# A fused state-space layer with a mixture of experts: both inverse roots of the row statistics in one step, those of the later chunks inside chunk 0, and a new table of places

## The reference, cut to what matters

```python
def layer(x):                        # x: (4, 1024, 256), fp32
    xn = layernorm(x)                # (x - mean) / sqrt(var + eps)
    return x + mamba(xn) + moe(xn)

def mamba(resid):                    # E = 512 channels, N = 16 states, R = 128
    rn = resid * rsqrt(mean(resid * resid) + EPS) * norm_w
    skip, x_in = rn @ skip_w.T, rn @ in_w.T
    x = silu(conv_b + causal_conv_4_taps(x_in, conv_w))
    delta = softplus(x @ wd1.T @ wd2.T + wd2_b)
    B, C = x @ wB.T, x @ wC.T
    h[l] = exp(delta[l] * A) * h[l-1] + (delta[l] * x[l]) * B[l]   # for each (e, n)
    y[l] = sum over n of h[l] * C[l]
    return resid + ((y + x * W_D) * silu(skip)) @ out_w.T

def moe(xf):                         # 8 experts, each token goes to 2 of them
    gates = softmax(xf @ Wr); scores, inds = the two smallest gates, normalised
    return sum of scores * ((silu(xf @ W1[e]) * (xf @ V1[e])) @ W2[e])
```

## Time and profile before

| | |
|---|---|
| median of 3 runs | 1356.34 us (1352.92 to 1358.64) |
| the profiled execution, its own time | 1352.63 us |
| its span | 1350.8 us |
| busy share of the span | DVE 87%, PE 83%, POOL 78%, ACT 75% |
| first scan of chunk 0, of chunk 1 | 50.86 us, 159.44 us |
| last scan ends | about 1335.9 us |

### The profile page before, as it was taken

One profiled execution on the slowest core, in us unless ns is written; L12 is line 12 of the kernel. 1 busy time (PEld: TensorE's weight loads), 2 busy tenths in 40 slices (PEclk: granted clock), 3 DMA queues, 4 the chain that ended last, 5 costly groups with the idle time before them and its releaser, 6 DMA issues.

```text
span 1350.8 us, 20706 instructions
## 1 busy us (share of the span) xinstructions
PE 1118.8 (83%) x5428; PEld 811.8 (60%) x5428; DVE 1176.3 (87%) x2147; ACT 1014.4 (75%) x2155; POOL 1054.3 (78%) x916
## 2 busy tenths in 40 slices
PE   4478476878889888889989898998989899898766
PEld 2367365655656665566666566666756666665555
DVE  5784999898989798999998899999989888989896
ACT  2898335678887887879788787978878787877863
POOL 1486278588887879789897988989888897978764
PEclk8666687789999998999999999999999999998888
DMA  7457623734444444445454354545435454434445
GB/s 215 147 194 250 249 87 87 243 127 132 135 134 145 119 141 128 133 123 149 135 141 130 120 151 127 144 135 136 139 117 144 134 140 138 134 114 129 124 139 178
DMA packets 87313, 195.37 MB, mean 145 GB/s; under 512 B 11216, under 2 KB 47312, under 8 KB 87120
## 3 DMA queue, kind: packets, MB, share of 16 engines
q1 hardware_dynamic: 69008, 171.18, 38.0%
q0 software_dynamic: 17904, 22.82, 10.3%
q10 hardware_dynamic: 288, 0.07, 0.0%
HBM read 171.36 MB, written 26.61 MB: 147 GB/s over the span
## 4 chain that ended last, share of the span: by engine, by line
PE 28%; POOL 21%; ACT 14%; issue 12%; DVE 7%; DMA 3%; DVEq 0%; POOLq 0%; ACTq 0%
POOL part L760 14%; PE yps L854 6%; ACT aexp L551 5%; PE bankX L1008 4%; PE bankH L974 4%; DVE hb L1116 4%; DVE bps L1095 3%; PE bankV L998 3%; PE bankG L879 2%; ACT tap L611 2%; POOL acc L815 2%; PE bankV L879 2%; DMA scr<-xt,idx 1%; POOL x L788 1%; POOL tap L789 1%
## 5 line engine op out<-in xcount | busy, mean ns | idle before, releaser
L760 POOL TENSOR_TENSOR part<-hb,bcr 128x512 f32<-128x512 f32 x512 | 694.2, 1406 | 188.3 <-PE yps L854 105.2
L1116 DVE TENSOR_TENSOR_SCAN hb<-aexp,carry,bps 128x256 f32<-128x256 f32 x768 | 547.3, 735 | 10.2 <-ACT aexp L551 7.8
L551 ACT ACTIVATE aexp<-delta,Am 128x256 f32<-128x256 f32 x1024 | 447.9, 505 | 35.8 <-DVE hb L1116 33.8
L854 PE MATMUL yps<-idn,part 128*128 128x128 f32 x2048 | 326.9, 292 | 141.2 <-POOL part L760 139.1
L854 PEld LDWEIGHTS yps<-idn,part 128*128 128x128 f32 x2048 | 251.6, 149 | 241.4 <-POOL part L760 180.5
L1095 DVE TENSOR_TENSOR bps<-ups,bcr 128x512 f32<-128x512 f32 x512 | 346.1, 676 | 5.1 <-DMA bcr<-brows 3.2
L1116 DVE TENSOR_TENSOR_SCAN hb<-aexp,bps 128x256 f32<-128x256 f32 x256 | 167.7, 674 | 14.8 <-ACT aexp L551 12.5
L974 PE MATMUL bankH<-w,scr 128*128 x288 | 148.1, 639 | 11.1 <-issue 8.1
L1008 PE MATMUL bankX<-w,scr 128*128 x576 | 145.0, 397 | 12.2 <-ACT scr L701 12.1
L998 PE MATMUL bankV<-v,scr 128*128 x288 | 136.8, 598 | 0.4 <-ACT tqO L656 0.4
L1008 PEld LDWEIGHTS bankX<-w,scr 128*128 128x128 f32 x576 | 108.8, 199 | 32.9 <-issue 19.4
(11 more groups left out here) (178 smaller groups left out, 1704.8 us busy)
## 6 DMA issues: line engine op xcount, KB each, us to landing
bcr<-brows SPq DMA_DIRECT2D x256, 512.0 KB
w<-in_W SPq DMA_DIRECT2D x2, 4096.0 KB, 20.9
xch<-in_x SPq DMA_DIRECT2D x16, 256.0 KB, 4.3
w<-in_x SPq DMA_DIRECT2D x4, 1024.0 KB, 10.5
xt<-scr SPq DMA_DIRECT2D x16, 256.0 KB, 2.8
acc<-scr SPq DMA_DIRECT2D x16, 256.0 KB, 2.8
v<-in_V SPq DMA_DIRECT2D x1, 4096.0 KB, 14.3
acc<-mst POOLq DMA_DIRECT2D x15, 256.0 KB
```

The lines of the kernel that those rows point to most:

```text
L551: nc.scalar.activation(aexp[:, w % EXP_SLOTS, i, :], delta[:, c % 2, e, :], ACT.Exp, scale=Am[:, e, n:n + 1]).then_inc(s_a, 1)
L760: nc.gpsimd.tensor_tensor(part[:, w % PART_SLOTS, :, :], hb[:, w % STATE_SLOTS, :, :], bcr[:, w % (2 * ROW_PAIRS), CH:2 * CH].unsqueeze(1) ...
L854: mm = pe.matmul(yps[:, s, i * P:(i + 1) * P], part[:, w % PART_SLOTS, i, s * P:(s + 1) * P], idn[:, :], start=(n == 0 and s == 0 and i == ...
L1116: v.tensor_tensor_scan(hb[:, w % STATE_SLOTS, i, :], aexp[:, w % EXP_SLOTS, i, :], bps[w % 2][:, i, :], first, ALU.mult, ALU.add).then_inc ...
```

## The change

The two inverse roots are now taken in one step. The inner norm's one is written as a function of the variance: `rs2[:, 0]` is the inverse root of var + eps, `rs2[:, 1]` that of var * (1 + eps) + eps * eps, so one Sqrt and one refinement on a tile twice as wide give both. The piece ST is split. BN, the moments of the 30 tiles, stays in the prologue, ahead of DL instead of behind it. The inverse roots of those tiles (ST) move to place 1 of chunk 0, and with them the Sqrt on ScalarE. A one-element Exp (`warm`) follows the first silu. DL of chunk 0 goes from GpSimd to VectorE. The projection of the B and C rows is a piece of its own, B5, behind B4; in the prologue as well. The router pieces have places from RA_FIRST on and reach into chunk 1, and the tables of places and of LATER change, most in chunks 0, 1 and 15.

```diff
-B_PIECES = [..., ("B3",), ("B4", 0), ("B4", 1), ("SP", 0), ("SP", 1), ("DL",)]
+B_PIECES = [..., ("B3",), ("B4", 0), ("B4", 1), ("B5",), ("SP", 0), ("SP", 1), ("DL",)]
...
-    "other": [3, 6, 7, 7, 12, 12, 12, 14, 14, 17, 17, 18, 22, 24, 24, 24, 27, 27],
+    "other": [3, 6, 7, 7, 12, 12, 12, 14, 14, 17, 17, 18, 22, 23, 23, 24, 24, 27, 27],
...
-    0: [0, 3, 4, 9, 10, 12, 13, 17, 20, 23, 25, 25, 25, 27, 27, 27, 27, 29],
+    0: [0, 3, 4, 9, 9, 12, 13, 17, 20, 24, 25, 26, 26, 26, 26, 26, 27, 27],
...
-RA_PLACES = [29, 29, 29, 30, 30, 30]
+RA_FIRST = 24
+RA_PLACES = {
+    "router": [6, 7, 7, 8, 8, 8],
+}
+ST_PLACE = 1
...
-DVE_DELTA = (2,)
+DVE_DELTA = (0, 2)
...
-    return [("B1", 0, 0)] + b2 + convs + x2 + [("B3", 0, 0), ("B4", 0, 0), ("B4", 1, 0), ("SP", 0, 0), ("SP", 1, 0), ("DL", 0, 0), ("ST",)]
+    return [("B1", 0, 0)] + b2 + convs + x2 + [("B3", 0, 0), ("B4", 0, 0), ("B4", 1, 0), ("B5", 0, 0), ("SP", 0, 0), ("SP", 1, 0), ("BN",), ("DL", 0, 0)]
...
-    "ACT": {"B4": 1, "SP": 1, "O2": 1, "B3": 2, "X2": 1, "B5": 1, "D": 1, "B2": 1},
+    "ACT": {"B4": 1, "SP": 1, "O2": 1, "X2": 1, "B5": 1, "D": 2, "B2": 1},
...
-                for step in (STAT_VAR, STAT_RMS):
-                    act.wait_ge(stat, step[g])
-                    nc.scalar.activation(sq[:, t0:t1], ta[:, t0:t1], ACT.Sqrt).then_inc(sact, 1)
-                act.wait_ge(stat, STAT_LN[g])
+                act.wait_ge(stat, STAT_VAR[g])
+                nc.scalar.activation(sq[:, :, t0:t1], ta[:, :, t0:t1], ACT.Sqrt).then_inc(sact, 1)
...
                     act.wait_ge(ld_xch[c % 2], 16 * (c // 2 + 1))
+                    if c < 2:
+                        act.wait_ge(stat, STAT_LN[c])
...
-                    nc.scalar.activation(dtT[:, :], bank["G"][:, 0:CH], ACT.Copy)
-                    act.wait_ge(conv, KE * (c + 1))
-                    nc.scalar.activation(brow, bank["G"][0:2 * N, CH:2 * CH], ACT.Copy).then_inc(free["G"], 1)
+                    nc.scalar.activation(dtT[:, :], bank["G"][:, 0:CH], ACT.Copy).then_inc(free["G"], 1)
+                elif kind == "B5":
+                    c = piece[2]
+                    wait_full(act, "G", piece)
+                    at_least(act, brow_w, 32 * c)
+                    act.wait_ge(conv, KE * (c + 1))
+                    nc.scalar.activation(brow, bank["G"][0:2 * N, 0:CH], ACT.Copy).then_inc(free["G"], 1)
...
+                if piece == ("X2", 0, 0):
+                    nc.scalar.activation(warm[:, :], db[:, 0:1], ACT.Exp)
...
+            def inverse_roots(g):
+
+                t0, t1 = GROUPS[g]
                 dve.wait_ge(bst, 2 * t1)
                 mean, var = mv[:, t0:t1, 0], mv[:, t0:t1, 1]
+                root, under, rs = (a[:, :, t0:t1] for a in (sq, ta, rs2))
+                link(v.tensor_scalar(under[:, 0, :], var, EPS, None, ALU.add))
+
+                link(v.tensor_scalar(under[:, 1, :], var, 1.0 + EPS, EPS * EPS, ALU.mult, ALU.add))
+                assert done[0] == STAT_VAR[g]
+                dve.wait_ge(sact, g + 1)
+                link(v.reciprocal(rs, root))
+                link(v.tensor_tensor(root, rs, rs, ALU.mult))
+                link(v.tensor_tensor(root, root, under, ALU.mult))
+                link(v.tensor_scalar(root, root, -0.5, 1.5, ALU.mult, ALU.add))
+                link(v.tensor_tensor(rs, rs, root, ALU.mult))
+                link(v.scalar_tensor_tensor(out=nm2[:, :, t0:t1], in0=mean.unsqueeze(1).to_broadcast([P, 2, t1 - t0]), scalar=-1.0, in1=rs,
+                                            op0=ALU.mult, op1=ALU.mult))
+                link(v.tensor_scalar(r1[:, t0:t1], rs[:, 0, :], 1.0, None, ALU.add))
```

## The result

The changed kernel took 1331.28 us (median of 4 runs, 1328.11 to 1333.41), the kernel before 1354.63 in the runs beside it (4 runs, 1352.24 to 1358.64). The ratio is 0.9824, 95% interval 0.9802 to 0.9845: 1.8% faster. The profiled execution took 1333.41 us, its span is 1331.6.

The account below looks back on a forecast made before the run. No single engine bounds the whole kernel (VectorE 87% busy, TensorE 83%); ScalarE bounds chunk 0. Terms 10.8 - 2.8 + 0.5 = 8.5 us give 1344.1 from the profiled 1352.63, 1347.8 from the median; forecast 1345, range 1332 to 1357.

Parts of the forecast that it names:

- The first statistics and the prologue: Before chunk 0's scans: statistics end 2.1 us earlier, ScalarE's exponentials start 10.8 us earlier, the first scan 9.8 earlier.
- What chunk 0 takes back: In chunk 0: a Sqrt and two table loads are new work on ScalarE, the bounding engine, costing 2.8 us.
- My upper bound of 6.3: Most that chunk 0 takes back: 2.8 + 2.2 + 1.3 us, adding VectorE's own instructions and one more load's halt.
- The end of chunk 0: Last R pieces to start of chunk 1: 4.1 us gained less 3.6 for later R pieces, net 0.5 us gained.
- RA's wait of 9.50: Before the router, VectorE waits 9.50 us for the last logits; RA one unit later was to fill it.
- the rival in which five R pieces in a row starve the scans: Chunk 0 loses the gain again through the R chain or GpSimd: 1352 us, chance 0.19.
- the 4 or more that I had made a condition: End of chunk 0: prediction is wrong if the last R piece is not earlier by 4 us or more.
- at most 4 gained, and as much lost: Chunk 1: same instructions, only about 4 us of VectorE's time idle, so counted 0, within 4 us either way.
- The rest: Chunks 1 to 15: counted at 0; chunks 2 to 14 keep the same work, bounded by 6 us either way.
- run in parallel: From chunk 2's first scan: traces keep their distance; a change above 6 us behind 254 makes the prediction wrong.
- The rival of slower steady chunks: At place 22 ScalarE waits for TensorE and VectorE runs dry, in each of 12 chunks: 1360 us, chance 0.10.
- The first rival: Chunk 0 hides the Sqrt and Ln, chunk 1 loses its few gaps: 18 us gained, 1335 us, chance 0.20.

Follow-up runs that it names:

- the kernel with the start alone: Kernel before with only the new statistics and prologue, B5 still inside B3, old places except chunk 1's B1: 1349.14 us, ratio 0.9962.

## Why the prediction was wrong

**The first statistics and the prologue: right.** First scan predicted 9.8 us earlier, measured 9.74. Each landmark that I named up to there is within 0.3 us.

**What chunk 0 takes back: 2.8 predicted, too small.** The roots inside chunk 0 cost some 4 us (the kernels with the roots in the prologue), and chunk 0 took back 5.1 in the kernel with the start alone. I priced ScalarE's two table loads and its Sqrt and gave VectorE's own instructions nothing, since it is busy only 70% there. They stand in its queue all the same: 2.98 us between two scans, with GpSimd and the R pieces behind. My upper bound of 6.3 had them. How the 4 us divide between the two engines was not tested.

**The end of chunk 0: near in its landmarks, wrong in its mechanism.** Last R copy 126.1 (near 125), RA without a wait, chunk 1 at 141.63 (near 140), unit 1 at 155.03 (near 153), chunk 2 at 246.31 (near 245). The gain of 8.5 that I had at chunk 2 was 7.8. But I had RA's wait of 9.50 filled and 4.1 us gained by it; VectorE stood still for 15.35 us in the burst instead, one unit earlier, as in the rival in which five R pieces in a row starve the scans. From the last R copy to the end of the first unit of chunk 1 it is 28.9 us (27.3 forecast, 31.4 before). And the last R copy is 3.9 us earlier, not the 4 or more that I had made a condition. That the sum came out near is in part luck.

**Unseen: 4.2 us lost in chunk 2.** Because everything at the end of chunk 1 moved, the first gather of the experts stands at place 30 instead of 28 and SP's 4 MB load is issued 0.2 us behind it instead of 7.5 us behind (250.65 against 243.18 before); the second gather lands in 7.0 us instead of 3.2. The kernel with the earlier gather shows that it is this: TensorE's wait is 7.2 us shorter in it, and chunk 3 starts 4.6 us earlier. My "at most 4 gained, and as much lost" for chunk 1 had no such mechanism, and I had not asked what the shifted places do to transfers.

**"The rest": the step that failed.** I wrote "In chunks 2 to 14 the work is the same. What moves is the copy of `dtT` on ScalarE" and "I cost it at nothing", with a bound of 6 us. Chunks 3 to 14 gained 16.1. The work was the same, but it was not only the copy that moved: B4 went from place 24 to 23, and three to six entries of each expert row moved by one to four places. I judged these by VectorE's wait for exponentials alone, 9.1 us in 984. That number was small, and yet 7.4 of it were one wait of 0.9 us repeated in each six-tile chunk, a wait that the order of one row could remove. And it was the wrong view for TensorE, which is busy just as long as VectorE in the earlier trace rows and waited 31.3 us for `part` and 12.1 for FB's copy in eight chunks. Had the steady chunks stayed as I said, the profiled time would have been 1352.63 - 3.6 = 1349: two errors of opposite sign, 15.5 us in the steady chunks and the last one, 4.9 us (8.5 less 3.6) ahead of chunk 3.

**The rivals.** None is what happened. The forecast that both traces "run in parallel" behind 254 was the condition by which I said the prediction would fall, and it fell by it. The rival of slower steady chunks had the right place (22 to 24) with the wrong sign: splitting the matmuls took a wait of the copy away (9.3 us before in eight chunks, 2.5 after) and put none in its place. The first rival's 1335 is the nearest number, but its reason, that chunk 0 takes back less than I counted, is not what the runs show.

**Two readings.** My stretch from 254 to 1238 holds 12.6 chunks, not 12.8, which changes nothing in the sum. And in my description of the change the tables change "most in chunks 0, 1 and 15"; counted by what they are worth, it was the rows of chunks 2 to 14.

**Left open.** Which of the numbers in the row of chunk 2 and that of five tiles are worth the 5.6 us (by the medians) between the kernel with all old expert rows and that with the six-tile row alone, and why chunk 14 gained 4.4 us, were not taken apart (with its old preparation row and the rest as changed, chunk 14 took 76.77 us, less than the 78.07 of the changed kernel). The new `LATER` always went with the split of B3 or the new places, so its own share is not known. Nor is the reason why "8, 8" is harmless and "14, 14" is not.

## What to carry to other kernels

When a change shifts entries in a hand-made order of a balanced pipeline, a row of places in a kind of chunk that repeats eight times deserves more of the working than the prologue: here one row cost 0.8 us in one chunk and more than the whole new start was worth in all. Whether two dependent pieces at one place do harm has to be read from the engine that they hold up: at place 14 the wait reached VectorE, at place 8 it did not. Read the waits of each engine that is near the bound by times as well as by total: a wait whose count is the number of chunks is an order that can be changed. And where small transfers are waited for, ask which large one is issued beside them after the shift. A landmark that comes out near says nothing of the wait behind it: look for the wait that you had promised to fill.

## What the runs showed of the hardware that I had not expected

A gather lands in 3.2 us when the load of 4 MB is issued 6 us behind it, and in 2.9 when it is issued 2.9 us behind. With the load 0.2 us behind the gather took 7.8 us, though it was issued first (one recorded landing, in the kernel with the old row of six tiles), and the next one, issued 1.2 us behind the load, took 7.0 in both the changed kernel and that one.
